# Gates and expert biases multiplied as stacks of bf16 parts, a padded transpose, and the turning of an attention set at a step's end, in a fused two-layer attention and mixture-of-experts kernel

## The reference

```
xn = layernorm(x)
x = x + attention(xn, Wq, Wk, Wv, Wo) + experts(xn, ...)
# layer 0: scores = xn @ W_gate + b_gate; the two largest are the weights w (0 for the others)
#          h = relu(xn W1[e] + b1[e]); y = h W2[e] + b2[e]; out = sum_e w[e] * y[e]
# layer 1: gates = softmax(xn @ Wg + bg); the two largest divided by their sum
#          out = sum over the two of gate * (xn We[e] + be[e]);  attention adds a bias bo
```

## Time and profile before

| | |
|---|---|
| time, median of 3 runs | 3337.09 us (3321.36 to 3341.45) |
| the profiled execution: time / span | 3337.99 us / 3336.3 us, granted clock 0.981 |
| PE busy | 3119.1 us (93%) |
| DVE busy | 2358.7 us (71%) |
| ACT busy | 1983.1 us (59%) |
| POOL busy | 1031.3 us (31%) |
| DMA | 149 GB/s over the span |

### The profile page before, as it was taken

How to read it: one execution, slowest core, us unless ns; L and a number is a source line. 1 busy time by engine, 2 the same in 40 slices (tenths; PEclk the granted TensorE clock), 3 DMA queues, 4 the chain that set the end, 5 groups by cost and what they waited for, 6 DMA issues and landing times.

```text
span 3336.3 us, 61910 instructions
## 1 busy us (share of the span) xinstructions
PE 3119.1 (93%) x19184; PEld 1605.8 (48%) x19184; DVE 2358.7 (71%) x7192; ACT 1983.1 (59%) x4954; POOL 1031.3 (31%) x1243
## 2 busy tenths in 40 slices
PE   4899999999999999999999999999999999999998
PEld 2554544444455554544445455444445545444443
DVE  4767677777776767778776676777777767677773
ACT  1566565656666666656566655666656666556664
POOL 4115133241422414233151331514233151331512
PEclk7999999999999999999999999999999999999998
DMA  8636354363554536345374553635446364453632
GB/s 230 209 115 209 109 168 138 103 177 113 173 167 146 177 116 181 111 137 166 98 213 124 180 152 118 190 90 165 146 132 193 120 197 128 149 146 93 187 111 70
DMA packets 315430, 496.16 MB, mean 149 GB/s; under 512 B 52960, under 2 KB 227040, under 8 KB 315104
## 3 DMA queue, kind: packets, MB, share of 16 engines
q1 hardware_dynamic: 281472, 417.56, 42.2%
q0 software_dynamic: 24576, 67.14, 6.5%
q10 hardware_dynamic: 9056, 7.49, 0.9%
HBM read 344.42 MB, written 152.84 MB: 149 GB/s over the span
## 4 chain that ended last, share of the span: by engine, by line
PE 74%; DVE 13%; ACT 5%; issue 5%; DMA 2%; POOL 1%; SPq 0%; ACTq 0%; DVEq 0%; POOLq 0%
PE po L1088 14%; PE pmx L1038 12%; PE pst L1025 10%; PE pst L1072 9%; PE pmx L1156 7%; PE pst L1057 4%; PE pmx L1125 4%; DVE pmx L806 3%; DVE rmax L802 3%; PE pst L1167 3%; PE pst L1046 3%; PE pmx L1122 3%; PE pmx L1106 2%; ACT probs L652 2%; ACT oraw L681 1%
## 5 line engine op out<-in xcount | busy, mean ns | idle before, releaser
L652 ACT ACTIVATE probs<-pst 128x512 f32<-128x512 f32 (+3 forms) x3072 | 1403.8, 496 | 528.5 <-PE pst L1025 519.3
L562 POOL TENSOR_SCALAR_AFFINE_SELECT probs<-probs 128x512 f32<-128x512 f32 x512 | 326.3, 637 | 1908.8 <-ACT probs L652 1906.4
L802 DVE TENSOR_REDUCE rmax<-pmx 128x1 f32<-128x512 f32 x1024 | 668.8, 683 | 144.8 <-PE pmx L1038 137.2
L1038 PE MATMUL pmx<-k_first,qs 96*128 96x512 bf16 (+2 forms) x2048 | 676.6, 345 | 45.5 <-DVE rmax L806 14.0
L1025 PE MATMUL pst<-qs,k_first 98*128 98x512 bf16 (+3 forms) x2048 | 685.6, 341 | 2.5 <-ACT probs L652 0.7
L806 DVE CUSTOM_DVE_ANT_0 pmx<-pmx,mask,rmax 128x128 f32<-128x128 f32 (+3 forms) x1024 | 535.1, 555 | 195.7 <-PE pmx L1038 188.0
L1088 PE MATMUL po<-probs,v 128*32 128x512 f32 (+3 forms) x6144 | 657.6, 499 | 6.1 <-POOL probs L562 6.1
L806 DVE CUSTOM_DVE_ANT_0 pmx<-pmx,mask 128x128 f32<-128x128 f32 (+3 forms) x1024 | 484.0, 509 | 147.5 <-PE pmx L1038 145.5
L1038 PEld LDWEIGHTS pmx<-k_first,qs 96*128 96x128 bf16 x2048 | 199.0, 98 | 438.5 <-issue 124.0
L1038 PE MATMUL pmx<-k_second,qs 96*128 96x128 bf16 (+3 forms) x1024 | 305.7, 303 | 27.5 <-DVE rmax L806 17.1
L1025 PE MATMUL pst<-qs,k_second 98*128 98x512 bf16 (+3 forms) x1024 | 300.7, 300 | 0.0
(11 more groups left out here) (111 smaller groups left out, 3695.3 us busy)
## 6 DMA issues: line engine op xcount, KB each, us to landing
wt<-w_tiles SPq DMA_DIRECT2D x184, 513.0 KB
qk_parts<-parts SPq DMA_DIRECT2D x256, 192.0 KB, 3.7
xg<-x_slots SPq DMA_DIRECT2D x368, 128.0 KB
y_slots<-ys SPq DMA_DIRECT2D x368, 128.0 KB
wt<-w_tiles SPq DMA_DIRECT2D x184, 256.0 KB
qs<-qk_parts SPq DMA_DIRECT2D x128, 192.0 KB
qs<-qk_parts SPq DMA_DIRECT2D x128, 128.0 KB
k_first<-qk_parts SPq DMA_DIRECT2D x64, 192.0 KB, 2.9
```

The lines of the kernel that those rows point to most:

```text
L562: pool.affine_select(out=tri, in_=tri, compare_op=ALU.is_ge, fill=0.0, base=0, pattern=[[0, GH], [1, P]], channel_multiplier=-1).then_inc( ...
L652: act.activation(probs[:, u % 2, j, 0:w], ps[:, 0:w], ACT.Exp, scale=DH ** -0.5).then_inc(st_read, 1)
L802: dve.tensor_reduce(rmax0[:, col:col + 1], src, AX_X, ALU.max).then_inc(mx_read, 1)
L1038: pe.matmul(bk[:, 0:b - a], qs[0:STACK, set_no(q, n) % QRING, j, t % HT * P:(t % HT + 1) * P], keys[0:STACK, j, 0:b - a], start=True, stop ...
```

## The change

1. The gates are split into three bf16 parts (high, middle, low) and the biases too. `gateT` and `wbias` each hold six blocks of 16 rows, which are paired as (0,0), (1,0), (0,1), (1,1), (0,2), (2,0): one bf16 matmul with 96 rows takes the place of one f32 matmul with 16 rows in `project_output`.
2. VectorE does the split of the gates in two new parts of `gates` (14 and 15, one at the end of step 26, the other behind the first maxima of step 27). `turn_gates` transposes eight bf16 pieces of 96 columns into one bank, and one copy takes them all.
3. The biases are loaded raw, split by VectorE once at the start (`split_biases`), and put under each other by twelve small DMAs on ScalarE's queue (`load_biases`, in step -30). SyncE waits for these before its first load of expert weights, since `wt` serves as scratch for it. The two loads of the old `wbias` go.
4. `mparts` has 128 columns, of which 96 stay zero, so its transpose has 128 columns of weights.
5. `turn_set` and `attention_output` stand at the end of the step, behind the fourth maxima and scores pieces. The transposed gates use one bank of the ring and not two, so from there on a piece has another bank.

```diff
+GATE_PARTS, BIAS_PARTS = (0, 1, 0, 1, 0, 2), (0, 0, 1, 1, 2, 0)
+GSTACK = 6 * GR
-GATE_PLACES = [0, 2, 3] + list(range(8, 19)) + list(range(24, 36))
+GATE_PLACES = [0, 2, 3] + list(range(8, 21)) + list(range(24, 36))
...
-        wbias = [sb(f"wbias{l}", [P, D]) for l in range(LAYERS)]
+        wbias = [sb(f"wbias{l}", [GSTACK, D], BF16) for l in range(LAYERS)]
-        gateT = sb("gateT", [GR, 2, T])
+        gateT = sb("gateT", [GSTACK, 2, T], BF16)
-        mparts = sb("mparts", [P, MROWS * GH * HT], BF16)
+        mparts = sb("mparts", [P, P], BF16)
+        gparts = sb("gparts", [P, NT, 6, GR], BF16)
...
+            def load_biases():
+                act.wait_ge(bias_split, 1)
+                for l in range(LAYERS):
+                    for b, m in enumerate(BIAS_PARTS):
+                        load(wbias[l][b * GR:(b + 1) * GR], bias_parts[:, m, l * D:(l + 1) * D], bias_loaded)
...
                 elif part == 14:
+                    dve.wait_ge(gate_ready, q + 1)
+                    link(dve.tensor_copy(gparts[:, :, 0:6:2, 0:E + 1], rows(gate).unsqueeze(2).broadcast_to([P, NT, 3, E + 1])))
+                    link(dve.tensor_tensor(rows(grest), rows(gate), gparts[:, :, 0, 0:E + 1], ALU.subtract))
+                elif part == 15:
+                    link(dve.tensor_copy(gparts[:, :, 1:5:2, 0:E + 1],
+                                         rows(grest).unsqueeze(2).broadcast_to([P, NT, 2, E + 1])))
+                    dve.tensor_tensor(gparts[:, :, 5, 0:E + 1], rows(grest), gparts[:, :, 1, 0:E + 1],
+                                      ALU.subtract).then_inc(gate_split, 1)
...
-                for c in range(CH):
-                    ps = full("gateT", q, c)
-                    dve.tensor_copy(gateT[:, q % 2, c * BANK:(c + 1) * BANK], ps[0:GR, :]).then_inc(mx_read, 1)
+                ps = full("gateT", q)
+                dve.tensor_copy(gateT[:, q % 2], ps[:].bitcast(BF16)[0:GSTACK]).then_inc(mx_read, 1)
...
-                        for q, n in set_ended(g):
-                            attention_output(q, n)
+                for q, n in set_ended(g):
+                    attention_output(q, n)
...
+            def split_biases():
+                dve.wait_ge(bias_raw_loaded, 16 * LAYERS)
+                link(dve.tensor_copy(bias_parts[:, 0], bias_raw))
+                link(dve.tensor_tensor(bias_rest, bias_raw, bias_parts[:, 0], ALU.subtract))
+                link(dve.tensor_copy(bias_parts[:, 1], bias_rest))
+                dve.tensor_tensor(bias_parts[:, 2], bias_rest, bias_parts[:, 1], ALU.subtract).then_inc(bias_split, 1)
...
-                pe.transpose(bk[:].bitcast(BF16)[0:MROWS * GH * HT, 0:P], mparts[:], identb[:]).then_inc(mx_full, 1)
+                pe.transpose(bk[:].bitcast(BF16)[:, 0:P], mparts[:], identb[:]).then_inc(mx_full, 1)
...
-                    pe.matmul(ps[:, t * D:(t + 1) * D], gateT[:, q % 2, tile * P:(tile + 1) * P], wbias[l][0:GR],
+                    pe.matmul(ps[:, t * D:(t + 1) * D], gateT[:, q % 2, tile * P:(tile + 1) * P], wbias[l][:],
                               start=(t == 0), stop=False, skip_group_check=True)
...
-                for t in range(HT):
-                    mm = pe.transpose(ps[0:GR, t * P:(t + 1) * P], gate[:, HT * c + t], ident[:])
+                for t in range(NT):
+                    mm = pe.transpose(ps[0:GSTACK, t * P:(t + 1) * P], gparts[:, t].rearrange("p a e -> p (a e)"), identb[:])
...
-                    if j == 2:
-                        for q, n in set_ended(g):
-                            turn_set(q, n)
+                for q, n in set_ended(g):
+                    turn_set(q, n)
```

More of the change, by code:

```diff
@@ L104 @@
 END = max(STORE) + 1
-PACK0, ATTENTION1, ORDER, PACK1 = -40, 1, (-35, 10), 4
+PACK0, ATTENTION1, ORDER, PACK1, BIASES = -40, 1, (-35, 10), 4, -30
 BEGIN = min(STATS[0])
@@ L199, in uses @@
                 st["hidden", *tile_hidden(g)] = len(st)
-            if j == 2:
-                for q, n in set_ended(g):
-                    mx["set", q, n] = len(mx)
+        for q, n in set_ended(g):
+            mx["set", q, n] = len(mx)
         for n, q in turns:
@@ L209, in uses @@
             mx["pos", q] = len(mx)
-            for c in range(CH):
-                mx["gateT", q, c] = len(mx)
+            mx["gateT", q] = len(mx)
     return mx, st
@@ L229, in attention_moe_kernel @@
         wo = [sb(f"wo{l}", [P, KD, D]) for l in range(LAYERS)]
-        wbias = [sb(f"wbias{l}", [P, D]) for l in range(LAYERS)]
+        wbias = [sb(f"wbias{l}", [GSTACK, D], BF16) for l in range(LAYERS)]
         bg = [sb(f"bg{l}", [P, E]) for l in range(LAYERS)]
         wt = sb("wt", [P, WRING, W_ALL])
+        bias_raw = wt[0:GR, 0, 0:LAYERS * D]
+        bias_rest = wt[0:GR, 1, 0:LAYERS * D]
+        bias_parts = wt[0:GR, 2, 0:3 * LAYERS * D // 2].bitcast(BF16).rearrange("p (m n) -> p m n", m=3)
         xg = sb("xg", [P, XRING, D])
@@ L331, in attention_moe_kernel @@
         gate_ready = sem("gate_ready")
+        gate_split = sem("gate_split")
+        bias_raw_loaded = sem("bias_raw_loaded")
+        bias_split = sem("bias_split")
+        bias_loaded = sem("bias_loaded")
         picks_ready = sem("picks_ready")
@@ L401, in load_attention @@
                 load(wo[l][:], A["wo"][l].rearrange("(k p) n -> p k n", p=P), w_attn[l])
-                load(wbias[l][:], A["wbias"][l], w_attn[l])
                 load(bg[l][:], A["bg"][l].partition_broadcast(P), w_attn[l])
@@ L476, in load_weights @@
                     sp.wait_ge(w_packed[l], 16 * (3 if l == 0 else 1) * E)
+                if m == 0:
+                    sp.wait_ge(bias_loaded, 16 * 6 * LAYERS)
                 if m >= WRING:
@@ L594, in _ @@
                 pool.memset(sums_col, 1.0)
-            for m in (mask, gate, earlier, before):
+            for m in (mask, gate, earlier, before, mparts, gparts):
                 link(pool.memset(m[:], 0.0))
@@ L748, in step @@
                         take_output(q, c, k)
+            for l in range(LAYERS):
+                load(bias_raw[:, l * D:(l + 1) * D], A["wbias"][l][0:GR], bias_raw_loaded)
             act.wait_ge(consts, 1)
@@ L755, in _ @@
                     pack_expert(0, g - PACK0)
+                if g == BIASES:
+                    load_biases()
                 if g == ATTENTION1:
@@ L814, in gates @@
                 value, picked = gs[:], gate[:, :, 0:E]
+                rows = lambda a: a[:, :, 0:E + 1]
                 other = value.unsqueeze(2).broadcast_to([P, NT, E, E])
@@ L876, in gates @@
                     link(ins)
-                elif part == 20:
+                elif part == 22:
                     with nc.allow_low_precision(reason="whole numbers below 4096"):
@@ L989, in order_weights @@
             def order_weights(l):
-                dve.wait_ge(w_attn[l], 96)
+                dve.wait_ge(w_attn[l], 80)
                 for m in range(2):
@@ L1000, in _ @@
                     order_weights(ORDER.index(g))
+                if g == ORDER[0]:
+                    split_biases()
                 step(g)
@@ L1116, in project_output @@
                 pe.wait_ge(st_read, st_done("oT", q, c, KD - 1))
-                pe.wait_ge(mx_read, mx_done("gateT", q, CH - 1))
+                pe.wait_ge(mx_read, mx_done("gateT", q))
+                if q in (0, LAYERS) and b == 0:
+                    pe.wait_ge(bias_loaded, 16 * 6 * LAYERS)
                 ps = mx("y", q, b)
@@ L1209, in step @@
                     find_places(q)
-                    for c in range(CH):
-                        turn_gates(q, c)
+                    turn_gates(q)
             for g in PROGRAM:
```

34 lines of the change are left out of this document (17 added, 17 removed).

## The result

| | before | after |
|---|---|---|
| time, median of 4 runs each | 3334.51 us (3321.36 to 3341.45) | 3230.57 us (3214.72 to 3239.26) |
| profiled execution, time / span | 3337.99 / 3336.3 us | 3239.26 / 3237.5 us |
| granted clock of the profiled execution | 0.981 | 0.979 |

The ratio is 0.9687, with a 95% interval of 0.9638 to 0.9737: 104 us less (88 to 121). The profiled execution of after is the longest of its four.

What follows compares the result with a forecast made beforehand. TensorE was taken to bound the kernel, with 74% of the chain. From 3337.99 us, bias products 90, set 30 and gates 7, less padding 6 and start 3, gave 118 us less: 3220 us, range 3185 to 3285.

Steps and rivals of the forecast that it cites:

- The bias products, 90 us: In TensorE's output products: 0.67 us saved per tile, 85 us, plus 6 us at entries, taken as 90.
- The 6 us at the entries: At the start of each of 64 output products: 0.09 us saved behind the preceding maxima matmul.
- the second rival: In output products: the extra load gap comes from f32 against bf16; 68 us instead of 90, 3242 us, chance 0.12.
- VectorE's cover: At output products: VectorE waits 135.8 us, 2.1 each, for TensorE, so 1.3 us shorter products still save time.
- The first rival: VectorE takes over where TensorE gets faster, half the products' gain and all the set's lost: 3290 us, chance 0.14.
- The gates, 7 us: Gate transposes and copies: 4 us saved on TensorE, 3 taken from VectorE's shorter copy; ends -8 and +12.
- The padding, 6 us lost: Turned maxima: 0.22 us to the transpose and 0.15 to attention, 0.05 more, 128 times; ends +11 and -18.
- The third rival: At the turned maxima: padding to 128 columns pays, total 3203 us; chance 0.10.
- The set, 30 us: Moving the set's turning to the step's end fills TensorE's stalls before the transposes of oraw; ends 0 and 43.
- what is late next ... That covers it: After the set's move: VectorE's later work is covered, since the next step's third maxima piece comes about 1.7 us later.
- just such a new wait: Sign of being wrong: a new wait of TensorE's maxima for otok; no size given.
- The start, 3 us: Twelve DMA issues on ScalarE's queue, 7.3 us, make the first copy and the first run's gates 3 us late; ends 0 and 8.

Runs made afterwards that it cites:

- stack_only: Kernel before plus only the bf16 stacks of gates and biases; turned maxima at 32 columns, set turned at its old place: 3252.50 us, ratio 0.9730.
- f32_128rows: Kernel before, with f32 bias products given 128 rows in place of 16, the added rows zero: 3298.52 us, ratio 0.9876.
- no_pad: Changed kernel with the turned maxima back at 32 columns: 3225.72 us, ratio 0.9642 to the kernel before.
- gates_earlier: Changed kernel with 32-column turned maxima and twelve pieces of VectorE's gate work one or two places earlier: 3197.05 us, ratio 0.9571 to the kernel before.

## Why the prediction came out as it did

3220 us was forecast, 3231 measured: 104 us less in place of 118, which the interval of 88 to 121 takes in. The mechanism held, and its largest term to a few us. Term by term:

- **The bias products, 90 us.** Right in the product, wrong in the entry. The 62 products of the trace became 84 us shorter, where 85 were forecast for 64. The 6 us at the entries did not come: 7 of 62 products have the 0.09, and all starts together gained 0.7 us. The step that failed is that one sample's entry was taken for all 64. stack_only, in which gates and start are also changed (94 forecast), gave 90. The bound of 68 us, the second rival, fell with f32_128rows: its rows are f32 next to bf16 at 0.22. The rule of the Trainium skill ("TensorEngine Tiling (Array Packing)", "Key Properties"), that a change of tiling mode drains TensorE, agrees with the four kernels that differ in it: the gap is there with 16 rows in f32 and in bf16, and gone with 96 and with 128.
- **VectorE's cover.** Right. Its wait for the products fell by 91.6 us, about as much as these became shorter, and 44.2 us of it are left, below the 60 that were named. The first rival, that half of the gain is lost to VectorE, did not come.
- **The gates, 7 us.** Right by the trace. TensorE saves 0.40 us in 16 places, 6 us where 4 were forecast. VectorE's copies fell from 20.5 to 11.0 us; the split takes 0.98 us (274 ns and three of 235 to 238; 1.14 forecast), 16 us in all, and its wait for the places' product fell from 16.0 to 8.3. That leaves VectorE 1 to 2 us better, where 3 were taken. No run has this part alone.
- **The padding, 6 us lost.** The cadences came as forecast, 0.22 and 0.15. As a cost it is smaller: 0 within 4 us alone. Beside the stacks and the moved set it isn't settled: between no_pad and the changed kernel are 5 us of the medians and 13 of the differences from the kernel before, with overlapping intervals, and at a granted clock of 0.981 the two took 3228.10 and 3226.80 us. The third rival, from the Trainium skill's "TensorE: Matmul & The Clock Gate", "Weight-path perf modes", that 128 columns load fast, is refuted as a gain here: attention next to the transpose has 32 columns, and the gap only moved.
- **The set, 30 us.** This is the term that was too large: 20 and 27 us in two pairs of kernels. The stall ahead of the transposes went as said (8.8 us left, below 10 forecast). What failed is the step "what is late next ... That covers it": the slack of 1.7 us was read in steps of ordinary load. Around steps 25 and 26 VectorE is late, and TensorE waits for `otok` there; the prediction had named just such a new wait as a sign of being wrong. From the view of waits, TensorE's for `otok` before and then after, with sum in us, times and longest:

```profile
PE pmx L1038 <- DVE otok L908: 8.9, 7, 1.3
```

```profile
PE pmx L1077 <- DVE otok L939: 17.3, 23, 1.0
```

  The prediction had the 7 waits of before, and took an eighth off for them; that they would be 23 it did not see.
- **The start, 3 us.** Too small: 4 to 6 us at the first attention, inside the bounds of 0 and 8. The 7.3 us of issues were right (7.6). The first copy itself was 2.7 to 6.1 us later, by trace, and not 3. As a term of the total it is not shown: with the issues out of the way, the time was no lower at the same clock.

So the terms that were too large are the set's, by 3 to 10 us, and the entry's, by about 5. The padding and the start, taken as 9 us of cost together, show as no loss of time that the runs can tell from none.

The changed kernel's profiled execution, 3239 us, is 9 us above its median. Where TensorE waits for VectorE's maxima ahead of a projection, the records of that projection run sometimes at full and sometimes at half speed. Two projections of this execution on TensorE's timeline, and the granted clock (the column behind the engines' busy times, 0.65 and 0.92) around the first:

```profile
677.15 3.65 PE L1197 MATMUL pmx<-xnT,wqk 128*128 128x512 f32 x4 [1.37 <-DVE rmax L827]
680.61 0.40 PE L1064 MATMUL pst<-qs,k_first 98*128 98x512 bf16 x1
...
3068.53 1.96 PE L1197 MATMUL pmx<-xnT,wqk 128*128 128x512 f32 x4 [1.71 <-DVE rmax L827]
3070.33 0.38 PE L1064 MATMUL pst<-qs,k_first 98*128 98x512 bf16 x1
```

```profile
676.00:680.00 4.00, 2.85 (x4) 1.24 (x5) 1.90 (x7) 0.46 (x1) 0.70 (x1) 0.65 0.40 115
680.00:684.00 4.00, 3.74 (x23) 1.34 (x22) 2.43 (x9) 3.04 (x7) 0.00 (x0) 0.92 0.00 0
```

3.46 us from start to start against 1.80. From 677.2 to 680.6 us the granted clock was 0.50, from 3068.6 to 3070.3 it was 1.00. In before, after, no_pad and gates_earlier there are 15 or 16 projections each that start over 1.5 us behind the record before them. Those among them that took over 3 us are 5 in before, 11 in after, 6 in no_pad and 5 in gates_earlier (no_pad and gates_earlier have one more each that was slow in part). 6 more at 1.7 us are 10 us, enough for what this execution has above the median; no other execution of the changed kernel has a trace to compare. Whether the change has a part in it isn't shown: no_pad, which has the same waits there, has 6.

## What to carry to other kernels

Read a matmul's cost from start to start and look at what shape stands next to it: the small product cost nearly as much by the gaps around it as by its own columns, and filling its rows with zeros alone removed almost half of what the whole change gained there. Before a step is moved, read its slack in the step where the other engine has the most to do; the gain of a move is what stays after that step's wait, and taking work out of that step can be worth as much (29 us here for one table of numbers, some 20 at the same granted clock) as the move. DMA issues in a compute engine's queue cost that engine their issue time (7.6 us for twelve here). And compare executions at the same granted clock before a difference of 10 us is given to an edit.

## What the runs showed of the hardware

- One bf16 record with 16 rows in a stream of full ones cost three gaps of about 0.1 us: ahead of it (0.31 against 0.216), behind it (0.19 to 0.21 against 0.11) and, where none had been expected, behind the first full record after it (0.32 against 0.216). In f32 the starts around 16-row records stood 0.30 to 0.32 apart against 0.216. Records with 96, 98 and 128 rows beside one another show no gap.
- A wait of TensorE of some 1.2 to 2.1 us ahead of a projection was followed in 5 to 11 of 15 or 16 cases by records at the lower of its two levels (1.2 of 2.4 GHz), 0.86 us for 512 f32 columns in place of 0.45, for all or most of the projection; in nearly all others by none. The runs of one kernel spread with that: those of the changed kernel took 3214.72 us at a mean granted clock of 0.986 and 3239.26 at 0.979.
- Small DMA issues took ScalarE 0.64 us each (eleven in 7.01 us), SyncE 0.61.
